# Kernel with the product in front of the sixth block: GpSimd waits for additions per three gathers and for each left-over sum where its block is overwritten

## What is computed

```
h = x @ W.T                      # after a layer norm of x; the kernel sums rows first, then multiplies
msg = h[src] * norm[:, None]
out = segment_sum(msg, dst, num_segments=n_nodes) + b
# layer 1: relu(out); layer 2: x + out; then logits = normalize(layernorm(x)) @ slots, softmaxes, experts
```

## Time and profile before

| | |
|---|---|
| median of 3 runs | 3066.69 us (3066.25 to 3067.5) |
| the profiled execution's own time | 3068.05 us |
| its span in the profile | 3066.3 us |
| mean granted clock of TensorE | 0.883 of full speed |
| busy, share of the span | PE 76%, POOL 60%, DVE 56%, PEld 47%, ACT 18% |

### The profile page before, as it was taken

The page is one execution under the profiler, slowest core; times in us unless marked ns, Lnnn a source line. Parts: engine busy times, 40 slices in busy tenths (PEclk is TensorE's granted clock), DMA queues, the critical chain, the costliest instruction groups (busy, mean ns, idle before and its releaser), DMA issues.

```text
span 3066.3 us, 28054 instructions
## 1 busy us (share of the span) xinstructions
PE 2329.3 (76%) x8202; PEld 1430.4 (47%) x8203; DVE 1712.4 (56%) x2249; ACT 541.4 (18%) x985; POOL 1844.9 (60%) x1857
## 2 busy tenths in 40 slices
PE   6626778777777777877757877888778788777888
PEld 6513444444444444444424544555445555444434
DVE  7645555555555555555535555555555555555416
ACT  7830110110011110110101111111111111111210
POOL 3357666666676666666556666666666666666000
PEclk9998898888888898888878888888888888889899
DMA  9498888888888888888668988888888888888737
GB/s 332 179 359 286 273 283 283 286 282 284 290 287 285 278 290 281 289 282 278 234 228 292 327 305 300 295 308 302 299 299 297 301 302 304 296 296 313 253 103 307
DMA packets 237825, 871.63 MB, mean 284 GB/s; under 512 B 64088, under 2 KB 64872, under 8 KB 237756
## 3 DMA queue, kind: packets, MB, share of 16 engines
q0 software_dynamic: 143808, 666.65, 62.9%
q1 hardware_dynamic: 66276, 162.56, 15.4%
q10 hardware_dynamic: 27692, 41.82, 3.7%
HBM read 826.10 MB, written 82.00 MB: 296 GB/s over the span
## 4 chain that ended last, share of the span: by engine, by line
PE 31%; issue 22%; DVE 20%; another core or an unknown queue 15%; ACT 5%; POOL 3%; DMA 3%; DVEq 1%; SPq 1%; ACTq 0%; POOLq 0%
PE work L1351 18%; DVE acc L1112 12%; PE left L1377 8%; DVE agg L1169 3%; POOL rows L674 2%; PE left L1429 2%; ACT acc L781 2%; DVE hid L1127 1%; DVE work L1131 1%; ACT logits L722 1%; ACT xsT L711 1%; DMA table_layer<-xstage 1%; DMA out_x<-xstage 1%; PE acc L1478 1%
## 5 line engine op out<-in xcount | busy, mean ns | idle before, releaser
L674 POOL DMA_INDIRECT rows<-table_layer,gidx x1764 | 1763.4, 1000 | 826.4 <-issue 497.2
L1351 PE MATMUL work<-WT,aggT 128*128 128x384 f32 x2352 | 892.4, 542 | 333.9 <-issue 276.8
L1112 DVE TENSOR_TENSOR acc<-acc,rows 128x768 f32<-128x768 f32 x1078 | 1038.5, 963 | 153.5 <-ACT acc L781 87.0
L1377 PE MATMUL left<-rows,hot 128*128 128x384 f32 x2352 | 939.7, 543 | 170.3 <-DVE agg L1169 100.7
L1351 PEld LDWEIGHTS work<-WT,aggT 128*128 128x128 f32 x2352 | 492.8, 213 | 732.7 <-issue 438.2
L1377 PEld LDWEIGHTS left<-rows,hot 128*128 128x128 f32 x2352 | 471.5, 211 | 485.0 <-issue 231.3
L1169 DVE TENSOR_TENSOR agg<-left,agg 128x768 f32<-128x768 f32 x98 | 93.9, 958 | 942.0 <-PE left L1377 470.8
L781 ACT ACTIVATE acc<-rows 128x768 f32<-128x768 f32 x98 | 79.8, 815 | 1316.7 <-DVE agg L1169 1224.7
L1363 PE MATMUL work<-sp_c,xsT 128*128 128x32 f32 x588 | 84.5, 265 | 75.9 <-issue 74.7
L811 ACT ACTIVATE aggT<-fixed 128x768 f32<-128x768 f32 x98 | 79.5, 811 | 275.7 <-issue 173.7
L1327 PEld LDWEIGHTS fixed<-ident,agg 128*128 128x128 f32 x588 | 101.5, 189 | 56.4 <-issue 47.7
(11 more groups left out here) (306 smaller groups left out, 1208.8 us busy)
## 6 DMA issues: line engine op xcount, KB each, us to landing
self_row<-table_layer SPq DMA_DIRECT2D x98, 384.0 KB
rows<-table_layer,gidx POOLq DMA_INDIRECT x1764
xstage<-in_x SPq DMA_DIRECT2D x67, 384.0 KB
xs<-in_x SPq DMA_DIRECT2D x58, 384.0 KB
table_layer<-ynext SPq DMA_DIRECT2D x49, 384.0 KB
xnew<-xs SPq DMA_DIRECT2D x49, 384.0 KB
table_layer<-xstage ACTq DMA_DIRECT2D x40, 384.0 KB
xstage<-xnew SPq DMA_DIRECT2D x21, 384.0 KB, 5.3
```

Of the source, the lines that this page charges most:

```text
L674: pool.indirect_dma_start(rows[:, slot, :], None, table[l][0:ROWS, :], bass.IndirectOffsetOnAxis(ap=gidx[:, k % 2, slot:slot + 1], axis=0) ...
L1112: dve.tensor_tensor(acc[:, :, 0:H] if n < OWN - 1 else halves(agg[:, :]), acc[:, :, 0:H], halves(row), ALU.add).then_inc(S["added"], 1)
L1351: m = pe.matmul(work[:, h, 0:H], aggT[:, kc, :], WT[l][:, kc, h * H:(h + 1) * H], start=kc == 0, stop=kc == KC - 1)
L1377: m = pe.matmul(left[:, h, 0:H], hot[:, b, c, :], rows[:, slot, h * H:(h + 1) * H], start=c == 0, stop=c == LEFT - 1)
```

## The change

GpSimd waits in six groups of three gathers instead of three groups of six (TRIPLES = 6 in place of BATCHES = 3). In front of group r it waits only for the additions of tile t-1 up to own block 2r+1 (`added` at least 12(t-1) + 2(r+1) - 1). In front of the left-over block 3r+1 it waits for that block's sum of tile t-1 alone (`left_summed` at least 6(t-1) + r + 1). Before, each batch of six waited for four additions more and two sums more at once. The gathers, their order, and everything on the other engines are the same.

```
-            per_own, per_left = OWN // BATCHES, LEFT // BATCHES
+            per_own = OWN // TRIPLES
...
-                    pool.reg_mov(summed_needed, LEFT * (PEELED - 1) + per_left)
+                    pool.reg_mov(summed_needed, LEFT * (PEELED - 1) + 1)
...
-                    for r in range(BATCHES):
+                    for r in range(TRIPLES):
                         if not known:
                             pool.wait_ge(S["added"], added_needed)
-                            pool.wait_ge(S["left_summed"], summed_needed)
                             pool.reg_add(added_needed, added_needed, per_own)
-                            pool.reg_add(summed_needed, summed_needed, per_left)
                         elif t >= 1:
                             pool.wait_ge(S["added"], OWN * (t - 1) + per_own * (r + 1) - 1)
-                            pool.wait_ge(S["left_summed"], LEFT * (t - 1) + per_left * (r + 1))
-                        for slot in range(r * CHUNKS // BATCHES, (r + 1) * CHUNKS // BATCHES):
+                        for slot in range(3 * r, 3 * r + 3):
+                            if slot == SLOT["left", r]:
+                                if not known:
+                                    pool.wait_ge(S["left_summed"], summed_needed)
+                                    pool.reg_add(summed_needed, summed_needed, 1)
+                                elif t >= 1:
+                                    pool.wait_ge(S["left_summed"], LEFT * (t - 1) + r + 1)
                             pool.indirect_dma_start(
```

More of the change, by code:

```diff
@@ L21 @@
 SLOT = {("own", c): 3 * (c // 2) + 2 * (c % 2) for c in range(OWN)} | {("left", c): 3 * c + 1 for c in range(LEFT)}
-BATCHES = 3
+TRIPLES = 6
 EXTRA = 28
```

## The result

The changed kernel takes 3075.67 us (median of 20 runs, 3060.13 to 3084.22), the kernel before beside it 3066.27 (20 runs, 3062.62 to 3069.35). The ratio is 1.0029, interval [1.002, 1.0038]: slower by 9.4 us, where 26 was forecast. Repeated on two other chips it was 1.0039 [1.0015, 1.0062] and 1.0035 [1.002, 1.005].

A forecast was written before the change was run, and what follows sets the result against it. GpSimd's gathers were taken to bound layer 2's loop and 25 of layer 1's 40 loop tiles. 13.5 + 7.5 + 5 = 26 us on 3068.05 gave 3094.1, less 1.36 for the median: 3093 us, range 3063 to 3115.

The forecast's parts named there:

- The late wait: Block 0's gather, now third behind the closing row, waits for the tile's first addition and starts 0.3 us late (bounds 0, 0.4).
- the long stop: GpSimd's wait for the sixth left-over sum, predicted to stand between the 18 gathers as before.
- From the late wait to the tile: Run's end and closing row both come 0.3 us later: 13.5 us in layer 2's 45 tiles, 7.5 in layer 1's 25.
- the reading: During a long unbroken run of gathers, completion of TensorE's last sums is seen only some 2.5 us after the run ends.
- the sign that the prediction named for its reading being wrong: Closing row closer to the last gather than 2 us while TensorE was done before.
- The stop moves: GpSimd's stop goes from block 12 to block 16, still a run of 18 gathers: worth 0 in a steady tile.
- The starts: Second and third tiles of a layer: GpSimd's run and the closing row end later, 5 us for both layers (bounds 0, 13).
- the sum's main term: The late start of block 0, passed on in full to the tiles of both layers: 13.5 + 7.5 us.
- The first rival: No change: early wait without latency, or GpSimd's end only goes with the closing row; 3067 us, at most 3073; chance 0.20.
- the rule that I weighed: DMA ports and engine ports cannot contend, so gathers would not hold TensorE's results: sum 0, time 3067 us.

The follow-up runs named there:

- e4: Changed kernel, but block 0's gather waits for the tile's fourth addition in place of the first: 3258.70 us, ratio 1.0558 to the kernel before.
- e9: Kernel before with 24 idle 128x128 products a tile on TensorE: 3781.74 us, ratio 1.2331 to the kernel before.
- e17: Kernel before with half-width gathers (half the data left out), on a chip with the delay: 3081.94 us, ratio 0.9998 to the kernel before.
- e5: The changed kernel once more, on a chip without the delay: 2904.21 us, ratio 1.0039 to the kernel before.
- e14: Kernel before with 40 one-column copies a tile on ScalarE in layer 2, ahead of the statistics: 2890.21 us, ratio 0.9999 to the kernel before.
- e15: Kernel before with half-width gathers (half the data left out), on a chip without the delay: 2888.68 us, ratio 0.9996 to the kernel before.
- e6: Changed kernel with additions waited for per three gathers, but left-over sums two per six gathers as before: 2890.08 us, ratio 1.0004 to the kernel before.
- e13: Kernel before with 24 idle products a tile on TensorE, each only 16 columns wide: 3074.55 us, ratio 1.0641 to the kernel before.
- e1: Changed kernel, but block 0 waits for ScalarE's copy, the addition is waited for at block 2: 3090.09 us, ratio 1.0034 to the kernel before.
- e2: Changed kernel with GpSimd's loop turned by half a tile, its branch back behind block 8: 3102.63 us, ratio 1.0068 to the kernel before.
- e3: Changed kernel with block 0 waiting for ScalarE's copy and GpSimd's loop turned by half a tile: 3091.91 us, ratio 1.0035 to the kernel before.
- e11: The changed kernel once more, on a chip with the delay: 3079.59 us, ratio 1.0035 to the kernel before.
- e8: Changed kernel with half-width gathers (half the data left out), a single execution: 2885.58 us.
- e10: Changed kernel with 24 idle 128x128 products a tile on TensorE: 3558.95 us, ratio 1.1614 to the kernel before.
- e16: Changed kernel with nine tiles ahead of each hardware loop in place of five: 2914.00 us, ratio 1.0084 to the kernel before.

## Why the prediction was off, by its own steps

- **The late wait: right.** 0.60 at the third gather, all others 0.30, the long stop in place; the start 3.60 behind the closing row was within what I gave.
- **From the late wait to the tile: this step failed.** It read: "the run ends 0.3 later, and by the reading above the closing row too". The first half held: on A the run of layer 2's tiles ends 0.32 later in the median. The second did not: the distance from the run's end to the closing row shrank from 2.54 to 2.31, which took back 0.23 of it. 0.3 was to be passed on in full in 70 tiles, 21 us; what came was 0.04 in 37 tiles of layer 2's loop and 0.06 in 37 of layer 1's, 4.0 us. That distance is no constant: the earlier trace rows had 3.61 already; tile 21 of the changed kernel has its closing row in mid run, which is the sign that the prediction named for its reading being wrong; e4 has such tiles too, and e4's 3.7 us more of waiting made 28.7 us tiles where the reading gives 32.8.
- **The reading itself: a symptom, not the rule.** On A, B, D and F TensorE's instructions are issued and completed slowly late in a run of gathers, and this ends 2.3 to 2.5 us after the run (e9, e17). In the steady tiles the closing row comes near that moment, as in the earlier trace rows; in others it gets through before, and in e9 it is not held at all. That a backlog decides between these I infer; no run varies it alone. Halving the bytes changes nothing (e17). On C (e5, the same program) and E (e14, e15) the delay isn't there. What it is that fills up between the two, and why on some chips only, stays open.
- **The stop moves: taken as 0, was 5 us.** The 5 us are tiles 16 and 32 of both layers, where GpSimd stalls. The stall was in the kernel before too: the records of GpSimd's sequencer put its branch back 5.30 behind the closing row there and 2.95 elsewhere (3.31 and 0.96 in the changed kernel). The gaps between gathers show nothing of it before, and I had looked at those alone. It shows where a stop has just let the sequencer lose its lead (e4, tiles 16 and 32), which the stop in front of block 16 does at the very gather where it falls. That the loss comes with the stop or the sums' waits and not with the additions' e6 shows for chip C alone (1.0004); there layer 1's tiles 16 and 32 take as long in e5 as in e6, so it tells nothing of the 5 us of A and D.
- **The starts: size right, place half right.** 5 forecast, bounds 0 and 13; layer 2's tiles 1 to 5 took 6.0 more, layer 1's none. Most of it lies in tiles 1 and 2, the second and third tile that the prediction names: 2.6 and 3.7 on A, 5.6 and -0.6 on D.
- **Not in the sum:** layer 1's last tiles, 2.9 less, the stretch between the layers 1.3 less, layer 2's last tiles 0.7 more.
- **Of what came, less than half is the sum's main term.** Of the 10.8 us between the traces 4.0 are the delay that was passed on, for which the sum had 21; 5.0 are the stall, for which it had 0; the other 1.8 are the stretches outside the loops.
- **The first rival was nearest.** It said that GpSimd's end goes with the closing row rather than holding it, and gave up to 3073, 3 short of the measured time; I gave it 0.20 on the ground that the earlier trace rows have runs that end at different places. But these differ in much else; none shows a run that ends 0.3 later with all the rest the same.

On the rule that I weighed, the Trainium skill (SBUF — State Buffer, "SBUF: two separate sides"), "PE, ACT, and DVE's dedicated pair never wait on anyone": chips C and E agree with it (0.10), A, B, D and F don't in effect (4.4 to 4.6), and since half the bytes change nothing, the delay need not be one of ports at all. Another page names a mechanism of this kind. The Trainium skill (NOTIFIC — the notification-queue block, "Overflow: three behaviours, one of which stalls the engine") says that the block's internal pipeline holds back its producers rather than lose a record, and that a nonzero count of such stalls would mean that an engine had been throttled. A path of records that is full would fit that they are missing on just the chips with the delay, though that sentence has none lost inside the block; no run here tests it.

## What to carry to other kernels

A completion that "follows" another engine's run at a constant distance in the steady state is company until a run moves that engine's end alone; price a delay of 0.3 us by such a run, not in full. When a stop moves, count how many queued instructions stand behind it: each stall of the sequencer that they covered is uncovered when they get fewer. And read the trace of TensorE behind the row that matters: three late logit products in the tile of the earlier trace rows would have said that more than the last sum was held. And read the time of the kernel before on more than one chip before trusting what bounds it: here two of six ran the same program 6% faster, with another bound in half of it. No version beat the kernel before; the finer waits for additions alone (e6) are level with it on the one chip where they ran.

## What the runs showed of the hardware that I had not expected

- The same kernel takes 2891 us on two chips and 3066 to 3085 on four. The changed kernel's tile of layer 2 is 23.4 on C against 26.5 on A and D, the closing row 0.1 against 4.5 behind TensorE's sum.
- On the four, TensorE issues one matmul in 0.7 to 2.1 us at times late in a run of gathers (before on A, e9, e17), and the traces lack a quarter to two fifths of the records of the program's counts, where those on C and E have all but two at most.
- A matmul of 16 columns takes as long as one of 128, 0.11 us at a granted clock of 1.00 and 0.21 at 0.50 (e9, e13).
- GpSimd's gathers stall once for 1.5 us at tiles 16 and 32 of both layers, in the changed kernel and in e1, e2, e3 and e11, at tile 16 of both in e4, and in layer 1 of e5, e8, e10 and e16; the cause is open.
